# A graph network on one core: the first layer's node rounds with x transposed by the host, eight PSUM banks and the bias on VectorE

## What is computed

```python
xl = (x @ Wl + bl).reshape(n, heads, outc)
e_feat = leaky_relu(xl[src] + (x @ Wr + br).reshape(n, heads, outc)[dst], 0.2)
logits = einsum('ehc,hc->eh', e_feat, att)
# softmax of the logits over the edges of each destination, then
out = segment_sum(xl[src] * a[:, :, None], dst)
```

## Time and profile before

| | |
|---|---|
| runs of the kernel | 7551.28, 7554.62, 7565.1 us; median 7554.62 |
| profiled execution | 7553.44 us, its span 7551.0 |
| PE / DVE / ACT / POOL busy | 5087.5 / 5192.5 / 4299.5 / 4698.4 us |
| mean granted TensorE clock | 0.717 |
| from the span's start to the first gather | 148.04 us |
| ten node rounds, first to last `n_made` | 62.13 to 139.91 us (starts of L1213) |

### The profile page before, as it was taken

One profiled execution on the slowest core, in us unless ns is written; L12 is line 12 of the kernel. 1 busy time (PEld: TensorE's weight loads), 2 busy tenths in 40 slices (PEclk: granted clock), 3 DMA queues, 4 the chain that ended last, 5 costly groups with the idle time before them and its releaser, 6 DMA issues.

```text
span 7551.0 us, 112829 instructions
## 1 busy us (share of the span) xinstructions
PE 5087.5 (67%) x25578; PEld 4133.6 (55%) x25578; DVE 5192.5 (69%) x16259; ACT 4299.5 (57%) x10701; POOL 4698.4 (62%) x4843
## 2 busy tenths in 40 slices
PE   5778787777888656666666666655665556565556
PEld 2666666666666545555454555545544445454544
DVE  3677777777777667777777777756666666666665
ACT  2555555555555456565655565645555555555546
POOL 1666666666666566666666666656666666666640
PEclk7777777777777766667767666667777777777766
DMA  4333333333333222222222222222222222222221
GB/s 129 89 97 96 89 97 97 98 98 97 89 96 97 73 61 63 63 63 63 63 63 62 63 63 63 63 50 58 58 59 59 58 58 58 58 58 58 58 54 46
DMA packets 416504, 544.50 MB, mean 72 GB/s; under 512 B 136173, under 2 KB 325155, under 8 KB 408365
## 3 DMA queue, kind: packets, MB, share of 16 engines
q0 software_dynamic: 154752, 327.15, 19.3%
q1 hardware_dynamic: 261549, 215.52, 10.2%
HBM read 483.66 MB, written 58.58 MB: 72 GB/s over the span
## 4 chain that ended last, share of the span: by engine, by line
DMA 35%; issue 30%; POOL 29%; PE 2%; DVE 2%; POOLq 1%; ACT 1%; SPq 0%; DVEq 0%; ACTq 0%
DMA xl_g<-xl_tab,edges 34%; POOL xl_g L714 29%; PE PS L883 1%; PE PS L742 1%; PE PS L809 0%; DMA ea<-state 0%; DVE ea L1174 0%; POOLq L710 0%; PE PS L741 0%; POOLq L713 0%; ACT msg L1047 0%; DMA digit_tab<-S 0%; POOLq L712 0%; PE PS L881 0%; DVE ea L1186 0%
## 5 line engine op out<-in xcount | busy, mean ns | idle before, releaser
L714 POOL DMA_INDIRECT xl_g<-xl_tab,edges x4836 | 4697.6, 971 | 2588.7 <-issue 1409.1
L809 PE MATMUL PS<-msg,S 128*128 128x137 f32 x9672 | 1697.7, 339 | 1170.0 <-DVE msg L1334 1169.1
L809 PEld LDWEIGHTS PS<-msg,S 128*128 128x128 f32 x9672 | 1541.7, 238 | 1316.3 <-issue 794.9
L782 PE MATMUL PS<-xr_w,ST 128*128 128x132 f32 x9672 | 1922.0, 359 | 127.2 <-DVE z L1235 92.3
L1235 DVE TENSOR_TENSOR z<-PS,xl_g 128x528 f32<-128x528 f32 x1302 | 865.0, 664 | 1596.4 <-DMA xl_g<-xl_tab,edges 1317.6
L782 PEld LDWEIGHTS PS<-xr_w,ST 128*128 128x128 f32 x9672 | 1733.3, 262 | 287.2 <-issue 151.8
L967 ACT ACTIVATE distT<-PS,neg_node 128x512 f32<-128x512 f32 x1302 | 843.4, 648 | 1560.7 <-PE PS L772 1556.5
L944 ACT ACTIVATE dist<-node_row,neg_dst 128x128 f32<-128x128 f32 x4836 | 1534.5, 386 | 0.0
L1242 DVE SCALAR_TENSOR_TENSOR am<-z,att_relu 128x512 f32<-128x512 f32 x1302 | 852.1, 654 | 34.5 <-issue 17.3
L947 ACT ACTIVATE S<-dist 128x512 f32<-128x512 f32 x1302 | 780.5, 599 | 41.1
L969 ACT ACTIVATE ST<-distT 128x512 f32<-128x512 f32 x1302 | 780.2, 599 | 41.5
(11 more groups left out here) (230 smaller groups left out, 3801.0 us busy)
## 6 DMA issues: line engine op xcount, KB each, us to landing
xl_g<-xl_tab,edges POOLq DMA_INDIRECT x4836, 2.6
ea<-edge_attr SPq DMA_DIRECT2D x62, 1248.0 KB, 6.9
xr_w<-xr_tab SPq DMA_DIRECT2D x186, 66.0 KB
dst_r<-dst_rows SPq DMA_DIRECT2D x186, 64.0 KB
node_row<-node_id SPq DMA_DIRECT2D x186, 64.0 KB
state<-t_new SPq DMA_DIRECT2D x126, 68.0 KB, 1.6
st_old<-state SPq DMA_DIRECT2D x124, 68.0 KB
state<-st_new SPq DMA_DIRECT2D x124, 68.0 KB
```

What stands on the lines that cost most here:

```text
L714: pool.indirect_dma_start(xl_g[:, q, t, :], None, xl_tab[stage][:, :], bass.IndirectOffsetOnAxis(idx[:, q, t:t + 1], 0))\
L782: last = pe.matmul(zp[(q + g) % 2][:, n, :], ST[:, t, :], xr_w[:, q, :], start=True, stop=True)
L809: last = pe.matmul(agg_ps, S[:, q, t, :], msg[:, t, :], start=t == 0 and stage > 0, stop=t == TILES - 1)
```

## The change

The host gives a second input `x_t`: for each round the 640 rows transposed, 128 x 640, in the order of the blocks. SyncE loads the first four rounds of it into `x_T` (X_BUFS = 4) between the weights of layer 1 and those of layers 2 and 3, and the bias rows of layer 1, broadcast to 128 partitions, into `b_row`; both `b_row` loads count in `weights_in`. TensorE has no transposes and no bias products in the rounds: one product a block into bank `block % 8`, waiting only for the bank to be read. VectorE adds `b_row` to a block out of PSUM into `n_lr` (five additions a round, `n_copied` now counts blocks) and goes on with the same five operations. ScalarE keeps only the copy to `n_new`. The wait for `n_stored` before `n_lr` is written stands on VectorE (and on ScalarE for `n_new`). The item table's load and the digit stores stand behind round 0's stores, the first two items' loads behind round 3's. On VectorE, the weight columns come ahead of the digits, and `b_parts` behind the rounds; `consts_made` is counted twice. The loops of rounds are written out. The later waits have BLOCKS = 50 in place of ROUNDS = 10 where they count blocks, and none for `n_T`, `n_Tc`.

```diff
+X_BUFS = 4
+BLOCKS = ROUNDS * NB
+        x_T = [ea_flat[:, q * NROWS:(q + 1) * NROWS] for q in range(X_BUFS)]
+        b_row = sb("b_row", [P, 2, XW])
-        WEIGHT_DMAS = 5 * LAYERS + 1
+        WEIGHT_DMAS = 5 * LAYERS + 3
 ...
         @block.sync
+            def load_x(r):
+                sp.dma_start(x_T[r % X_BUFS], x_t[r]).then_inc(x_loaded[r % X_BUFS], 16)
 ...
+                if l == 0:
+                    for s, b in enumerate((bl, br)):
+                        sp.dma_start(b_row[:, s, 0:F], b[0].partition_broadcast(P)).then_inc(weights_in, 16)
+                    for r in range(X_BUFS):
+                        load_x(r)
 ...
+            for r in range(ROUNDS):
+                store_round(r)
+                if r + X_BUFS < ROUNDS:
+                    load_x(r + X_BUFS)
+                if r == 0:
+                    sp.wait_ge(table_out, 112)
+                    sp.dma_start(tab[:, :], item_tab.rearrange("(a k) w -> a (k w)", a=1)).then_inc(table_in, 16)
+                    sp.wait_ge(digits_made, 4)
+                    sp.sem_inc(spacer, 1)
+                    for w in range(2):
+                        sp.dma_start(digit_tab[w].rearrange("c (h e) -> (c h) e", h=2), all_digits[w]).then_inc(digits_out, 16)
+                if r == 3:
+                    sp.wait_ge(table_in, 16)
+                    sp.sem_inc(spacer, 1)
+                    sp.wait_ge(digits_out, 32)
+                    windows.extend(load_item(q, q, 0, with_window=False) for q in range(2))
 ...
         @block.tensor
-                for j in range(NB):
-                    last = pe.transpose(hT_ps[:, j * P:(j + 1) * P], n_in[q][:, j, :], ident[:, :])
-                last.then_inc(n_T, 1)
-                pe.wait_ge(n_Tc, r + 1)
-                for j in range(NB):
-                    pe.matmul(lr_ps[:, j, :], ones_h[:, :], b_parts[:, 0, :, :].rearrange("a s f -> a (s f)"), start=True, stop=False)
-                    last = pe.matmul(lr_ps[:, j, :], n_hT[:, j * P:(j + 1) * P], w_lr[:, 0, :, :].rearrange("p s f -> p (s f)"),
-                                     start=False, stop=True)
-                last.then_inc(n_prod, 1)
+            for r in range(ROUNDS):
+                pe.wait_ge(x_loaded[r % X_BUFS], 16 * (r // X_BUFS + 1))
+                for j in range(NB):
+                    block = r * NB + j
+                    if block >= 8:
+                        pe.wait_ge(n_copied, block - 7)
+                    pe.matmul(PS[:, block % 8, 0:2 * XW], x_T[r % X_BUFS][:, j * P:(j + 1) * P], w_lr[:, 0, :, :].rearrange("p s f -> p (s f)"),
+                              start=True, stop=True).then_inc(n_prod, 1)
+            pe.wait_ge(consts_made, 2)
 ...
         @block.scalar
-                    act.copy(n_lr[q].rearrange("p j s f -> p j (s f)"), lr_ps).then_inc(n_copied, 1)
-                    act.copy(n_hT[:, :], hT_ps).then_inc(n_Tc, 1)
 ...
         @block.vector
+                dve.wait_ge(n_stored[q], use * stored_value)
+                dve.sem_inc(spacer, 1)
+                for j in range(NB):
+                    dve.wait_ge(n_prod, r * NB + j + 1)
+                    dve.tensor_tensor(out=n_lr[q][:, j, :, :].rearrange("p s f -> p (s f)"), in0=PS[:, (r * NB + j) % 8, 0:2 * XW],
+                                      in1=b_row[:, :, :].rearrange("p s f -> p (s f)"), op=ALU.add).then_inc(n_copied, 1)
+                dve.wait_ge(n_copied, (r + 1) * NB)
```

More of the change, by code:

```diff
@@ L527, in _ @@
                     sp.dma_start(xl_tab[l][at:at + P, :], t_new[:, 0:XW]).then_inc(table_out, 16)
[L528 to L534, removed]
@@ L535, in _, with load_round @@
             pairs = sp.value_load(pairs_i[0:1, 1:2], min_val=MIN_PAIRS, max_val=MAX_PAIRS)
             last_pair = sp.value_load(pairs_i[0:1, 2:3], min_val=MIN_PAIRS - 1, max_val=MAX_PAIRS - 1)
-            def load_round(stage, at):
+            def load_round(at):
                 r, q, use = at
[L541 to L564, removed]
+                sp.dma_start(n_x[q], rounds_of(x, r)).then_inc(fx_loaded[q], 16)
@@ new lines, in load_round, with store_round @@
+                sp.dma_start(n_st[q][:, :, 0:ROW_L], rounds_of(state[LAYERS - 1], r)).then_inc(st_loaded[q], 16)
+                sp.dma_start(n_st[q][:, :, ROW_L:ROW], rounds_of(state[0], r)[:, :, ROW_L:ROW]).then_inc(st_loaded[q], 16)
+            def store_round(r):
+                q = r % 2
+                sp.wait_ge(n_made, r + 1)
+                sp.dma_start(rounds_of(xl_tab[0], r), n_lr[q][:, :, 0, :]).then_inc(n_stored[q], 16)
+                sp.dma_start(rounds_of(xr_tab[0], r), n_lr[q][:, :, 1, :]).then_inc(n_stored[q], 16)
+                sp.wait_ge(n_first, r + 1)
+                sp.dma_start(rounds_of(state[0], r), n_new[:, q, :, :]).then_inc(n_stored[q], 16)
@@ L664, in last_step @@
                         sp.wait_ge(x1_ready, behind[0] + 1)
-                    load_round(LAYERS, ahead)
+                    load_round(ahead)
             rounds(sp, (0, 2), last_step)
@@ L899, in squares_of @@
                 return last
[L901 to L905, removed]
-                    act.copy(n_lr[q].rearrange("p j s f -> p j (s f)"), lr_ps).then_inc(n_copied, 1)
-                if ahead:
-                    act.wait_ge(n_T, ahead[0] + 1)
-                    act.copy(n_hT[:, :], hT_ps).then_inc(n_Tc, 1)
[L910 to L914, removed]
+            for r in range(ROUNDS):
+                q = r % 2
+                act.wait_ge(n_stored[q], (r // 2 + 1) * stored_value)
+                act.sem_inc(spacer, 1)
+                act.wait_ge(n_copied, (r + 1) * NB)
+                act.copy(n_new[:, q, :, C_ACC:C_ACC + F], n_lr[q][:, :, 0, 0:F]).then_inc(n_first, 1)
             act.wait_ge(consts_in, 16 * CONST_DMAS)
@@ L1447, in edge_step @@
                         turn_norm()
-            rounds(dve, (0,), lambda at: loop_logits(0, at))
+            for r in range(ROUNDS):
+                node_logits(0, (r, r % 2, r // 2 + 1))
+            dve.memset(ones_h[:, :], 1.0)
+            for whole, parts in ((b_lr.rearrange("a l s f -> a (l s f)"), b_parts[:, :, :, :].rearrange("a l s f -> a (l s f)")),
+                                 (b2_r[:, :], b2_parts[:, :])):
+                rest, left, part = whole, b_rest[:, 0:whole.shape[1]], b_cut[:, 0:whole.shape[1]]
+                for w in range(PARTS):
+                    here = ident[0:PARTS, w:w + 1]
+                    ch.link(dve.tensor_copy(part, rest))
+                    if w == 0:
+                        ch.link(dve.tensor_scalar(parts, part, here, None, ALU.mult))
+                    else:
+                        ch.link(dve.scalar_tensor_tensor(parts, part, here, parts, ALU.mult, ALU.add))
+                    if w < PARTS - 1:
+                        ch.link(dve.tensor_tensor(out=left, in0=rest, in1=part, op=ALU.subtract))
+                        rest = left
+            dve.sem_inc(consts_made, 1)
             dve.wait_ge(consts_in, 16 * CONST_DMAS)
```

73 lines of the change are left out of this document (27 added, 46 removed).

## The result

| | before | changed |
|---|---|---|
| median of six runs each, us | 7553.4 | 7508.27 |
| profiled execution / its span | 7553.44 / 7551.0 | 7503.96 / 7502.0 |
| first gather | 148.04 | 120.46 |
| stage 1 (first gather to the next stage's first) | 2468.8 | 2463.4 |
| stage 2 | 2367.2 | 2356.7 |

The ratio is 0.9937, 95% interval 0.9924 to 0.995: faster by 0.6%. The spans differ by 49.0 us. 27.6 of it is the head, as forecast in kind (31.5); 21.4 lies where the prediction had nothing, behind the first gather.

A forecast was written before the change was run, and what follows sets the result against it. GpSimd, issuing and awaiting its gathers, was taken as the bound, so only time before the first gather counts. The last `n_made` moves from 140.1 to 108.6, 31.5 us less: 7553.4 - 31.5 = 7522, range 7506 to 7538.

The forecast's parts named there:

- the head: The 148.04 us before the first gather; all the gain was expected there, 31.5 us less.
- The change leaves the gather loop as it is: Edge stages: GpSimd's gather loop stays as it was, 7403 us from its first gather, so only earlier work counts.
- rival 4: Edge stages' waits shift by themselves over 186 items; 0.2 us each would be 37 us, either way; chance 0.03.
- The weights: Setup: all weights land at 24.5 us, bounds 21 to 29, where VectorE found them at 20.64 before.
- the additions: Node rounds on VectorE: five bias additions out of PSUM at 0.40 us each, 2.0 a round.
- the stores' cycle of 5.9: Node rounds: with two buffers, two rounds take at least 11.75 us because of their stores, 5.9 each.
- the stall before round 3: Round 1's stores queue behind the digit stores on four engines, so round 3, reusing that buffer, stalls 12.2 us once.
- the items' loads: After round 3 SyncE issues two items' loads, 5.9 us; round 4's stores go out 2.8 late and round 6 waits.
- with the DMA share near 0.25 in it: Expected sign: during VectorE's wait of some 12 us before round 3's additions, the DMA share is near 0.25.
- 1 (digit stores hold nobody up): Node rounds: digit stores delay nothing or finish in half the time; about 7509 us; chance 0.22.
- 2: Slow digit stores plus late weights or slower additions eat the gain to within 0.2%; 7539 us or more; chance 0.07.
- 3 (stores become the bound): Node rounds: DMA rate falls; slower from 10.9 us a round on, 7568 us at 12.5 a round; chance 0.03.

The follow-up runs named there:

- fourth chip: Undisturbed chip of the last runs: the kernel before, unaltered, took 7587.15 us (one run); the changed kernel, unaltered, 7540.48, ratio 0.9957.
- group 2: Four variants run on one undisturbed chip, where the kernel before took 7582.83 us; neither kernel was profiled unaltered there.
- a_pad165q: Changed kernel with 165 semaphore increments more in VectorE's setup, second run, on an undisturbed chip: 7549.55 us, ratio 0.9959.
- b_pad96f: Kernel before with 96 semaphore increments more on VectorE ahead of its first work: 7574.11 us, ratio 0.9998.
- b_pad60f: Kernel before with 60 semaphore increments more on VectorE ahead of its first work: 7600.49 us, ratio 1.0032.
- the first group: Both kernels, unaltered and with spacing on VectorE, on a disturbed chip; the changed kernel unaltered took 8138.5 us, ratio 0.9984.
- a_split: Changed kernel with each of the two 124-row digit stores cut into 112 and 12 rows: 7535.91 us, ratio 0.9935.
- b_third: Kernel before, unaltered, profiled on a disturbed chip, where the kernel before took 8148.14 us.

## Why the prediction was wrong, and where it was right

**The step that failed** is "The change leaves the gather loop as it is", and with it "a gather loop that isn't 7403 us long from its first gather says rival 4": it was 7381.5. On the fourth chip it was 7439.9 before and 7414.4 after, 25.5 less. Rival 4 had 0.03 and was costed as chance. Its place in the program, named there and given no cost, counted: the profile of before shows 181 instruction packets in its part 3, and I did not ask in which stage they fell, nor why VectorE's `run_up` had 80.6 us of "issue" in stage 2 and 6.2 in stage 1. With 10.5 for stage 2, the head as it came and nothing else, the time would be 7553.4 - 27.6 - 10.5 = 7515, inside the range. But the timed runs bear out at most about 8 of the 10.5 as the price of the packets, so it is not shown that all of stage 2's gain is theirs.

The other 10.9 us (5.4 in stage 1, 1.7 in stage 3, 3.7 at the end) have no cause shown. On the fourth chip they came as 5.2, 0.3 and 3.0. Stage 1 varies by 12.4 within group 2 without a reason seen. The end is shorter after than before in all four pairs of unaltered kernels, by 3.0 to 6.8. It doesn't go with VectorE's place in the program: 260.2 in `a_pad165q`, which lies as the kernel before, 260.6 in `b_pad96f`, 266.4 in `b_pad60f`. "Nothing in the loop changed but its place in the program" isn't quite so either. Counted in the two programs, the bodies of stages 1 and 2 have one instruction more on ScalarE (151 to 152) and two more on SyncE (99 to 101 and 91 to 93), with the changed constants of their waits; VectorE's and GpSimd's are as long as before. No run tests what these do.

**The head**, 31.5 forecast, 27.6 measured in this pair, 27.9 in the first group. The weights (24.5 / 24.26), the first product (33.2 / 33.17), the start of round 0 (37.2 / 36.85), the additions (0.40 a block, 2.0 a round / 1.79), the stores' cycle of 5.9 and the stall before round 3 (12.2 / 12.22) are right. The 0.40 was partly luck: two thirds of 0.71 halved and one third kept give 0.47, and 0.36 was measured (1.79 for five). The 1.9 us for completion in the weights' sum is 1.7 by its own row, which would have given 24.3. `n_made` of round 5 came at 82.83 + 0.18, forecast 83.2; of the last 112.20 + 0.18, forecast 108.6.

**Mis-sized: the items' loads**, "5.9 with the reads of the table, so round 4's stores go out 2.8 late". From the end of round 3's issues (73.93) to the first store of round 4 (82.18) SyncE needs 8.25, because the reads of the table, 2.9 us, come ahead of the first load and had stood elsewhere in the row that I took. The stores went out 6.5 late, round 6 waited 7.33, and the 3.8 us by which the last `n_made` is late arise there: round 5 was on time, round 6 came at 95.14 where 91.1 was forecast.

**Right in sum, wrong in how it looks:** "with the DMA share near 0.25 in it". It was 0.43 to 0.49, then 0.73, 0.27 and 0.9 or more. I had the four slow engines, and not that SyncE's own issue stops behind them (4.32 and 5.45 us), so that x and round 2 come in late and together. That the sum came out at 12.2 all the same was partly luck.

**Rivals.** 1 (digit stores hold nobody up): refuted, 12.22, and `a_split` shows what it would have been worth, 8.8 at that wait and 5.2 at the first gather. 2: no. 3 (stores become the bound): they are what rounds wait for, at about 6.0 a round, far from the 10.9 at which it would cost. 4: happened, on the good side. It could have gone the other way: 60 instructions more instead of 91 clear stage 2 and cost stage 1 22 to 31 us, as `b_pad60f` shows for the kernel before.

## What to carry to other kernels

An edit far from a loop moves the loop's place in its engine's program. Look at part 3 of the page for instruction packets, in which stretch they fall, and at a once-a-pass "issue" wait at the top of the loop; where the body is a little longer than 256 instructions, as the two here, its place decided whether instructions came in again every pass. Spacing ahead of it moves that and can be tried; here it gave the kernel before no gain clear of noise, and in the wrong amount it cost 0.3%. Leave no DMA of 124 rows in a queue that others need: 112 + 12 took 9 us off one wait here and 5 off the first gather. And when a group of DMAs is moved on SyncE, count the register reads ahead of it.

## What the hardware showed that I had not expected

- The fetches cost VectorE 2.9 us a pass in stage 2 (80.6 / 28) and 6 in stage 1 (171.6 / 28). VectorE had slack for most of it, and the kernel lost much less. The Trainium skill (Runtime: NRT & Kernel Launch, "Instruction fetch mechanics") calls crossing a block mostly hidden and warns of jumps; the runs bear out the warning.
- A DMA on a quarter of the engines can hold up the engine that issues: behind the digit stores SyncE's issue took 5.45 us, and 0.65 with the same stores cut into 112 and 12 rows.
- The kernel before had its first gather anywhere from 144.94 to 158.13, the changed one from 120.46 to 123.48 (unaltered copies, all chips). TensorE's pair of product instructions takes 1.25 us or 0.71 in the kernel before, and its rounds 9.6 or 6.3 with them. In `b_third` all nine rounds that I could see took about 9.5, in `before` two took 6.3. The row of the second kind from the trace of before, then one of `b_third`:

```profile
103.05 0.71 PE L742 MATMUL PS<-w_lr,n_hT 128*128 128x264 f32 x2
```

```profile
80.50 1.25 PE L742 MATMUL PS<-w_lr,n_hT 128*128 128x264 f32 x2
```

  The clock column of the windows doesn't follow them at this grain: it shows 1.00 for 60 to 100 in `b_third`. The changed rounds wait for stores and hardly depend on it. So the head gained 21.5 to 36.8 us, mostly by how TensorE ran in the kernel before.
